# One scan instruction over two rows of states in a two-layer sequence model, with decays in PSUM and SBUF

## The chip, the cores and the metric

The kernel runs on one core of a Trainium2 chip. A core has five engines that run their own instruction streams and meet at semaphores: TensorE (matmuls and transposes, into PSUM), VectorE, ScalarE, GpSimd (no access to PSUM) and SyncE, which here only issues DMAs. The metric is the device time of one execution in microseconds (us). It is given as the median of three runs; the traces come from one profiled execution, whose own time stands beside its span.

## The reference, cut to what matters

Eight sequences of 1024 tokens with 512 features go through a conditioned linear-attention layer (layer 0) and then a conditioned state-space layer (layer 1). The change is in layer 1 alone. There the rows are gathered by a list of indices that lie, with these inputs, all below 512, so only the first 512 positions of each sequence have to be computed (the branch `first_chunk`). The core of the layer, for each sequence, 1024 inner channels d and 16 states s:

```python
A = -jnp.exp(A_log)                                  # [1024, 16]
dt = jax.nn.softplus(dtr @ W_dt + b_dt)              # [t, 1024]
def step(hst, inp):
    dt_t, B_t, C_t, x_t = inp
    dA = jnp.exp(dt_t[:, :, None] * A)               # the decay
    hst = hst * dA + (dt_t * x_t)[:, :, None] * B_t[:, None, :]
    y = jnp.einsum('bds,bs->bd', hst, C_t)
    return (hst, y)
...
y = jnp.transpose(ys, (1, 0, 2)) + xm * D_param
y = y * jax.nn.silu(z)
return y @ W_out
```

## The kernel before

Layer 0 takes the first third of the time and is not touched. In layer 1 the inner channels lie on partitions in eight groups j of 128, the 512 time steps lie along the free dimension. A **row** is one (j, s) pair, 128 partitions by 512 steps; a batch has 8 x 16 = 128 rows, and a **unit** U is four rows that share s and the half of the j. There are 32 units in a batch and 256 in all. `n` counts rows within a batch, `N` rows in all.

What is done for one row or unit:

- **Multiply** (GpSimd, `inputs`, L1866): the products (dt x)B of a unit's four rows in one operation of 128x2048, written to a place of the ring `hs` of four units (`RING = 4`). It waits until TensorE has turned all tiles of the unit four back (`turned`).
- **Decay** (ScalarE, `decays`, L1673): one Exp of 128x512 for each row, into one of three PSUM banks (`decay_banks`, banks 3 to 5), three rows ahead of the scan; it waits until the scan three rows back is done.
- **Scan** (VectorE, `scan`, L2029): the recurrence over 512 steps, in place in `hs`, with the decay from its PSUM bank. One instruction for each row.
- **Turn** (TensorE, `states_turned`, L1435): tile t of a unit is four 128x128 transposes that bring 128 time steps onto the partitions, into one of two PSUM banks. Tile t needs that tile t-2 was read.
- **Add** (VectorE, `add_states`, L2047, for tiles 0 to 2): multiply by C and add to `acc`. Tile 3 is scaled by ScalarE (`scale_state`, L1689) and added by a DMA that GpSimd issues (`pool_state`, L1904). `DVE_TILES = 3` sets this split.

The order on each engine is written out by hand: the function `turn(b)` of each engine runs over the 128 steps `n` and does at each one its part for row or tile `n`, and between them what other stages need at fixed steps (`XM_AT`, `DT_AT`, `Y_AT`, ...): the projections of the next batch, their taps (VectorE, L1997), SiLU and softplus on ScalarE, the gates, and a part of layer 0's output projection (`W_AT`), whose tiles come through `h_in` (three places). VectorE's adds run one step behind (`LAG = 1`), so in the unit of steps 4u to 4u+3 it scans unit u and adds the tiles of unit u-1. For each half batch GpSimd's queue has two more operations of 128x2048: L1847 (dt) and L1857 (dt times x).

The products of the other stages go through three **work banks** (6, 7 and 2), claimed in the order of `batch_places`. ScalarE computes softplus as an Exp and a Ln; Exp, Ln and SiLU are each in another set of tables, and a load of a set (`ACT_TABLE_LOAD`) is put ahead of an operation whose set is not there. `x_turned` (L1430) multiplies x by a diagonal matrix of D, eight of which VectorE makes once at the layer's start (L2187).

## Time and profile before

| | us |
|---|---|
| median of 3 runs | 3135.99 |
| lowest and highest | 3134.64, 3136.06 |
| the profiled execution, its own time | 3136.52 |
| its span in the trace | 3134.7 |
| busy: TensorE, VectorE, GpSimd, ScalarE | 2724.0, 2404.3, 1868.2, 1615.8 |
| first and last scan start | 1086.8, 3075.3 |

A busy time is the time in which an engine has an instruction under way. In the rows, a group has its busy time in us and the mean duration of one in ns, then the engine's idle time just ahead of the group and what ended it (the releaser). In a timeline the second number is the duration of the entry; an instruction's record may start while the one ahead of it is finishing, so two that run back to back overlap a little. "PE" is TensorE, "DVE" VectorE, "ACT" ScalarE, "POOL" GpSimd.

### The profile page before, as it was taken

To read this page: it belongs to the slowest core of one execution; us is meant where nothing else is said; L and a number is where in the kernel's file an instruction comes from. 1 tells how busy PE (TensorE), PEld (TensorE's weight loads), DVE (VectorE), ACT (ScalarE), POOL (GpSimd) and SP (SyncE) were. 2 spreads that over 40 slices of the span, in tenths; PEclk is the share of its full clock that TensorE was granted. 3 is DMA by queue.
4 is the path that set the end of the run, shared out by engine and by line. 5 is a ranking of instruction groups with operands and counts; after the bars stand their busy time and mean duration, and the time that the engine had idled before them with its cause. 6 is when DMAs were issued, how large, how long until landed. Compare 5 with 4: busy or idle time off the path is not lost. (4 is left out here: it accounts for less than half of the span.)

```text
span 3134.7 us, 32596 instructions
## 1 busy us (share of the span) xinstructions
PE 2724.0 (87%) x11066; PEld 1530.8 (49%) x11066; DVE 2404.3 (77%) x3090; ACT 1615.8 (52%) x2336; POOL 1868.2 (60%) x821
## 2 busy tenths in 40 slices
PE   7999999999999777988978888887897897888974
PEld 3556466456555344554544454444454454445542
DVE  3455445455544499989999999989998999999993
ACT  1222123223322466775775766776676577577550
POOL 0112111212113186887897898798799798789892
PEclk9999999999999778989989989999999998998976
DMA  6012022212215344454664664565566466456563
GB/s 207 7 54 74 27 101 88 88 54 89 85 65 164 107 96 99 108 118 114 142 154 104 152 152 105 140 157 112 128 158 132 105 157 142 111 139 144 146 136 72
DMA packets 261595, 355.28 MB, mean 113 GB/s; under 512 B 21597, under 2 KB 115937, under 8 KB 261434
## 3 DMA queue, kind: packets, MB, share of 16 engines
q1 hardware_dynamic: 202200, 246.46, 25.6%
q0 software_dynamic: 55680, 105.93, 19.6%
q8 instruction: 84, 1.38, 0.2%
q10 hardware_dynamic: 3554, 0.88, 0.1%
q14 instruction: 77, 0.63, 0.1%
HBM read 215.56 MB, written 71.58 MB: 92 GB/s over the span
## 5 line engine op out<-in xcount | busy, mean ns | idle before, releaser
L1866 POOL TENSOR_TENSOR hs<-slots,b_wide 128x2048 f32<-128x2048 f32 x256 | 1227.3, 4806 | 322.0 <-PE bank L1435 244.5
L2029 DVE TENSOR_TENSOR_SCAN hs<-bank,hs 128x512 f32<-128x512 f32 x1024 | 1219.7, 1208 | 48.5 <-ACT bank L1673 43.9
L1673 ACT ACTIVATE bank<-dt,decay 128x512 f32<-128x512 f32 x1024 | 700.4, 692 | 570.3 <-DVE hs L2029 568.9
L1435 PE MATMUL bank<-ident,hs 128*128 128x128 f32 x4096 | 681.1, 294 | 310.4 <-DVE acc L2047 240.8
L1435 PEld LDWEIGHTS bank<-ident,hs 128*128 128x128 f32 x4096 | 507.1, 150 | 848.0 <-DVE acc L2047 319.5
L2047 DVE SCALAR_TENSOR_TENSOR acc<-bank,c_t,acc 128x512 f32<-128x512 f32 x772 | 560.9, 727 | 62.7 <-PE bank L1435 60.6
L1388 PE MATMUL bank<-h_t,w_in 128*128 128x512 f32 x1024 | 509.3, 604 | 1.0 <-ACT h_t L1600 1.0
L1904 POOL DMA_DIRECT2D acc<-scaled x252 | 270.3, 1073 | 31.5 <-DMA acc<-scaled 19.3
L1483 PE MATMUL bank<-w_y,zs 128*128 128x512 f32 x512 | 253.0, 600 | 0.8 <-DVE zs L2148 0.8
L1399 PE MATMUL bank<-w_out,h_in 128*128 128x512 f32 x448 | 234.2, 649 | 1.3 <-ACT dt L1647 1.3
L711 PE MATMUL bank<-z_t,w_k 128*128 128x512 f32 x512 | 221.2, 592 | 0.9 <-ACT z_t L810 0.9
L711 PE MATMUL bank<-rows,z_t 128*128 128x512 f32 x512 | 221.1, 592 | 0.0
L711 PE MATMUL bank<-w_v,z_t 128*128 128x512 f32 x512 | 221.0, 592 | 0.0
L1388 PEld LDWEIGHTS bank<-h_t,w_in 128*128 128x128 f32 x1024 | 169.7, 194 | 82.6 <-issue 82.6
L868 POOL TENSOR_TENSOR x_rs<-x_var,mhalf 128x8 f32<-128x8 f32 x7 | 11.5, 1647 | 330.8 <-DVE x_var L298 330.8
L1689 ACT ACTIVATE scaled<-bank,c_t 128x512 f32<-128x512 f32 x252 | 169.7, 674 | 50.1 <-PE bank L1435 40.8
L873 POOL TENSOR_TENSOR qy<-qy,q_top 128x512 f32<-128x512 f32 x64 | 68.8, 1075 | 185.8 <-DVE q_top L945 185.8
L861 POOL TENSOR_TENSOR y_rs<-y_var,mhalf 128x8 f32<-128x8 f32 x8 | 15.9, 1992 | 254.6 <-DVE y_var L298 254.6
L813 ACT ACTIVATE k_t<-k_t,k_top 128x1024 f32<-128x1024 f32 x32 | 36.8, 1149 | 250.0 <-DVE k_top L915 250.0
L1997 DVE SCALAR_TENSOR_TENSOR slots<-bank,taps,slots 128x511 f32<-128x511 f32 (+2 forms) x192 | 142.1, 740 | 22.4 <-ACT slots L1613 19.9
L711 PEld LDWEIGHTS bank<-w_v,z_t 128*128 128x128 f32 x512 | 97.3, 190 | 122.5 <-issue 122.5
L711 PEld LDWEIGHTS bank<-z_t,w_k 128*128 128x128 f32 x512 | 96.7, 190 | 119.8 <-issue 118.6
(160 smaller groups left out, 3171.3 us busy)
## 6 DMA issues: line engine op xcount, KB each, us to landing
b_wide<-b_rows SPq DMA_DIRECT2D x256, 256.0 KB, 3.6
acc<-scaled POOLq DMA_DIRECT2D x252, 256.0 KB, 4.9
w_in<-in_L_cond_W_in SPq DMA_DIRECT2D x128, 256.0 KB, 3.3
z<-in_x SPq DMA_DIRECT2D x8, 2048.0 KB, 8.8
res<-in_x SPq DMA_DIRECT2D x8, 2048.0 KB, 9.7
h_tiles<-h_t SPq DMA_DIRECT2D x56, 256.0 KB, 3.4
h_in<-h_tiles SPq DMA_DIRECT2D x56, 256.0 KB, 4.8
x_rows<-w_part POOLq DMA_DIRECT2D x28, 512.0 KB, 8.9
```

What stands on the lines that cost most here:

```text
L711: last = nc.tensor.matmul(out[:, :], stationary(k), moving(k), start=(k == 0), stop=(k == blocks - 1))
L1388: last = nc.tensor.matmul(work_bank(place, stage, m)[:, :], w_in[:, m % W_IN_RING, k, :], h_t[:, place.par, k, :], start=(k == 0), stop=(k ...
L1399: last = nc.tensor.matmul(work_bank(place, "W", i)[:, :], h_in[:, w % W_RING, k, :], g.w_out[:, k, :], start=(k == 0), stop=(k == KD - 1))
L1435: last = nc.tensor.transpose(bank[:, j * P:(j + 1) * P], hs[:, slot, j, t * P:(t + 1) * P], ident[:, :])
L1483: last = nc.tensor.matmul(work_bank(place, "out", t)[:, :], zs[:, j, t * P:(t + 1) * P], w_y[:, j, :], start=(j == 0), stop=(j == KI - 1))
L1673: nc.scalar.activation(decay_banks[N % 3][:, :], dt[:, H % 2, j, :], ACT.Exp, scale=g.decay[:, 4 * (H % 2) + j, s:s + 1]).then_inc(da_read ...
L1689: nc.scalar.activation(scaled[:, U % SCALED_RING, t - DVE_TILES, :], state_banks[t % 2][:, :], ACT.Copy, scale=c_t[:, U // UNITS % 2, t, U ...
L1866: nc.gpsimd.tensor_tensor(hs[:, U % RING, :, :], slots[:, H % SLOTS, :, :], b_wide[:, U % B_RING, :].unsqueeze(1).to_broadcast([P, 4, CHUNK]),
L1904: nc.gpsimd.dma_start(acc[:, U // STATE % 2, DVE_TILES:, :], scaled[:, U % SCALED_RING, :, :], accum_op=ALU.add).then_inc(state_pooled, DMA)
L1997: nc.vector.scalar_tensor_tensor(row[:, back:], bank[:, 0:CHUNK - back], w, row[:, back:], ALU.mult, ALU.add).then_inc(empties(place, "xm" ...
L2029: nc.vector.tensor_tensor_scan(block, decay_banks[N % 3][:, :], block, 0.0, ALU.mult, ALU.add).then_inc(scanned, 1)
L2047: nc.vector.scalar_tensor_tensor(part, state_banks[t % 2][:, :], scale, part, ALU.mult, ALU.add).then_inc(summed, 1)
```

## The change

- **Paired scan.** `scan_pair` replaces `scan` in `turn`: one instruction over two neighbouring rows, 128x1024, at even steps. So that the second row starts from zero, the decay at each row's first step is zero: `clear_first` writes these zeros once, and `decays` writes elements 1 to 511 of each row only.
- **Decays in two pairs.** Rows 0 and 1 of a unit take their decays from a PSUM tensor of two banks (banks 3 and 4), rows 2 and 3 from `decay_pair` in SBUF. ScalarE runs four rows ahead (`LEAD`), and a row's decay is written once the pair two back is scanned.
- **Common tables.** After each SiLU the set that has both Exp and Ln is loaded at once; Exp and Ln then need no load between them.
- **Fourth work bank.** Bank 5 joins the work banks.
- **Room in SBUF.** Only two D diagonals are kept (`DIAG_RING`); ScalarE makes each again for every batch (`diagonal`, at `DIAG_AT`), and `x_turned` waits for it. `h_in` has two places in place of three, and its loads (`H_IN_AT`) are issued later.
- `tiles_of` now reads a table, with `THREE_TILES = 16`; as `U % STATE` is always below 16 it returns 3 as before, and the extra wait in `pool_state` never applies.

The diff, cut to its core:

```diff
+THREE_TILES = 16
+LEAD = 4
-W_RING = 3
+DIAG_RING = 2
+W_RING = 2
+DIAG_AT = (100, 103, 112, 114, 120, 122, 17, 20)
-H_IN_AT = (-1, 2, 5, 7, 24, 27, 30, 31)
+H_IN_AT = (3, 5, 7, 8, 27, 30, 31, 32)
...
-    places = [Place(b, b, b % 2, 2 * b, 0, {}, 3) for b in range(BATCH)]
+    places = [Place(b, b, b % 2, 2 * b, 0, {}, 4) for b in range(BATCH)]
...
+    return 3 if U % STATE < THREE_TILES else 2
...
+        decay_sb = sb("decay_pair", [P, 2 * CHUNK])
-        state_banks, decay_banks, work_banks = banks[0:2], banks[3:6], [banks[6], banks[7], banks[2]]
+        state_banks, decay_banks, work_banks = banks[0:2], banks[3:6], [banks[6], banks[7], banks[2], banks[5]]
+        decay_pairs = [g.decay_pair[:, :], decay_sb[:, :]]
...
             def x_turned(place, j):
                 out = claimed(pe, place, "init", j)
+                need(pe, d_ready, KI * place.it + j + 1)
...
-                    need(pe, scanned, 4 * (U + 1))
+                    need(pe, scanned, 2 * (U + 1))
...
+            def exp_and_log_tables():
+                nc.scalar.preload_act_table_set("natural_log_exp_and_others")
+            def diagonal(j):
+                nc.scalar.activation(d_diag[:, j % DIAG_RING, :], ident[:, :], ACT.Copy, scale=column(g, "L1_cond_D_param", j)).then_inc(d_ready, 1)
...
-                need(act, scanned, N - 2)
-                nc.scalar.activation(decay_banks[N % 3][:, :], dt[:, H % 2, j, :], ACT.Exp,
+                need(act, scanned, N // 2 - 1)
+                at = N % 2 * CHUNK
+                nc.scalar.activation(decay_pairs[N // 2 % 2][:, at + 1:at + CHUNK], dt[:, H % 2, j, 1:], ACT.Exp,
                                      scale=g.decay[:, 4 * (H % 2) + j, s:s + 1]).then_inc(da_ready, 1)
...
-                    if N + 3 < BLOCKS * BATCH:
-                        decays(N + 3)
+                    if N + LEAD < BLOCKS * BATCH:
+                        decays(N + LEAD)
...
+            def clear_first():
+                for pair in decay_pairs:
+                    nc.vector.memset(pair.rearrange("p (r t) -> p r t", t=CHUNK)[:, :, 0:1], 0.0).then_inc(first_cleared, 1)
+            def scan_pair(N):
+                need(dve, da_ready, N + 2)
                 if N % 4 == 0:
                     need(dve, inputs_ready, N // 4 + 1)
-                block = hs[:, N // 4 % RING, N % 4, :]
-                nc.vector.tensor_tensor_scan(block, decay_banks[N % 3][:, :], block, 0.0, ALU.mult, ALU.add).then_inc(scanned, 1)
+                rows = hs[:, N // 4 % RING, N % 4:N % 4 + 2, :].rearrange("p r t -> p (r t)")
+                nc.vector.tensor_tensor_scan(rows, decay_pairs[N // 2 % 2], rows, 0.0, ALU.mult, ALU.add).then_inc(scanned, 1)
...
-                    scan(N)
+                    if n % 2 == 0:
+                        scan_pair(N)
...
-                nc.vector.tensor_scalar(d_diag[:, j, :], ident[:, :], column(g, "L1_cond_D_param", j), None, ALU.mult).then_inc(d_ready, 1)
```

VectorE's order in a stretch of the first batches' scans where little stands between, before (`hs<-bank,hs` is a scan, `acc<-...` an add; the listing prints a scan under another operation's name):

```order
L2047 SCALAR_TENSOR_TENSOR acc<-bank,c_t,acc 128x512
L2029 SCALAR_TENSOR_TENSOR hs<-bank,hs 128x512 x2
L2047 SCALAR_TENSOR_TENSOR acc<-bank,c_t,acc 128x512
L2029 SCALAR_TENSOR_TENSOR hs<-bank,hs 128x512
L2047 SCALAR_TENSOR_TENSOR acc<-bank,c_t,acc 128x512
L2029 SCALAR_TENSOR_TENSOR hs<-bank,hs 128x512
L2047 SCALAR_TENSOR_TENSOR acc<-bank,c_t,acc 128x512
L2029 SCALAR_TENSOR_TENSOR hs<-bank,hs 128x512 x2
```

The same engine after, with the scans of 1024 elements from `bank` and from `decay_pair` in turn:

```order
L2080 SCALAR_TENSOR_TENSOR hs<-decay_pair,hs 128x1024
L2098 SCALAR_TENSOR_TENSOR acc<-bank,c_t,acc 128x512 x2
L2080 SCALAR_TENSOR_TENSOR hs<-bank,hs 128x1024
L2098 SCALAR_TENSOR_TENSOR acc<-bank,c_t,acc 128x512
L2080 SCALAR_TENSOR_TENSOR hs<-decay_pair,hs 128x1024
L2098 SCALAR_TENSOR_TENSOR acc<-bank,c_t,acc 128x512 x2
```

A unit was scan, scan, add, scan, add, scan, add; it is now a pair, an add, a pair and two adds.

ScalarE around the Exp (L1653) and Ln (L1658) of softplus, before:

```order
L1673 ACTIVATE bank<-dt,decay 128x512
L1625 COPY zs<-bank 128x512
L1673 ACTIVATE bank<-dt,decay 128x512
L1658 ACT_TABLE_LOAD
L1658 ACTIVATE dt<-dt 128x2048
L1673 ACT_TABLE_LOAD
L1673 ACTIVATE bank<-dt,decay 128x512 x2
```

and after, where they are L1674 and L1679:

```order
L1715 ACTIVATE scaled<-bank,c_t 128x512
L1699 ACTIVATE bank<-dt,decay 128x511
L1683 ACTIVATE d_diag<-ident,cols 128x128
L1643 COPY zs<-bank 128x512
L1699 ACTIVATE bank<-dt,decay 128x511
L1679 ACTIVATE dt<-dt 128x2048
L1699 ACTIVATE decay_pair<-dt,decay 128x511 x2
L1715 ACTIVATE scaled<-bank,c_t 128x512
```

The two table loads around Ln are gone, a diagonal stands between the copies, and the decays come in twos for a bank and for `decay_pair`.

## Rows read from the trace of the kernel before

**Rows 1.** Busy time in one stretch: us, PE, PEld, DVE, ACT, POOL.

```profile
1290.00:2790.00 1500.00, 1276.36 (x5429) 713.79 (x5430) 1414.31 (x1606) 1019.71 (x1444) 1258.15 (x501) 0.95 0.57 132
```

**Rows 2.** The page's costliest groups: the multiply and the decays.

```profile
L1866 POOL TENSOR_TENSOR hs<-slots,b_wide 128x2048 f32<-128x2048 f32 x256 | 1227.3, 4806 | 322.0 <-PE bank L1435 244.5
...
L1673 ACT ACTIVATE bank<-dt,decay 128x512 f32<-128x512 f32 x1024 | 700.4, 692 | 570.3 <-DVE hs L2029 568.9
```

**Rows 3.** Waits in 1290 to 2790: total us, times, longest.

```profile
POOL hs L1866 <- PE bank L1435: 193.9, 98, 3.5
...
DVE acc L2047 <- PE bank L1435: 44.7, 44, 3.1
DVE hs L2029 <- ACT bank L1673: 34.3, 36, 2.2
```

**Rows 4.** All scans (ns min/median/max); scans, then multiplies, in the stretch.

```profile
L2029 DVE TENSOR_TENSOR_SCAN hs<-bank,hs x1024: 1184/1210/1225, 1086.8 to 3075.3; 128x512 f32<-128x512 f32 x171
...
1290.00:2790.00 1500.00, 903.65 (x760) 0.95 0.57 132
...
1290.00:2790.00 1500.00, 903.50 (x190) 0.95 0.57 132
```

**Rows 5.** Timeline of VectorE: start us, us, instruction.

```profile
1208.06 1.21 DVE L2029 TENSOR_TENSOR_SCAN hs<-bank,hs 128x512 f32<-128x512 f32 x1
1209.19 0.73 DVE L2047 SCALAR_TENSOR_TENSOR acc<-bank,c_t,acc 128x512 f32<-128x512 f32 x1
1209.83 1.21 DVE L2029 TENSOR_TENSOR_SCAN hs<-bank,hs 128x512 f32<-128x512 f32 x1
```

**Rows 6.** Timeline of TensorE, GpSimd and VectorE at two adds of tile 1.

```profile
1209.97 1.11 PE L1435 MATMUL bank<-ident,hs 128*128 128x128 f32 x4 [0.66 <-DVE acc L2047]
...
1206.73 0.88 POOL L1904 DMA_DIRECT2D acc<-scaled  x1
1211.24 4.51 POOL L1866 TENSOR_TENSOR hs<-slots,b_wide 128x2048 f32<-128x2048 f32 x1 [3.64 <-PE bank L1435]
...
1117.23 0.72 DVE L2047 SCALAR_TENSOR_TENSOR acc<-bank,c_t,acc 128x512 f32<-128x512 f32 x1
...
1118.00 0.66 PE L1435 MATMUL bank<-ident,hs 128*128 128x128 f32 x4 [2.11 <-DVE acc L2047]
...
1118.82 4.55 POOL L1866 TENSOR_TENSOR hs<-slots,b_wide 128x2048 f32<-128x2048 f32 x1 [1.78 <-PE bank L1435]
```

**Rows 7.** L371, all and one, with the GpSimd operation beside it.

```profile
L371 DVE SCALAR_TENSOR_TENSOR shift<-mv,rs x7: 1101/4464/4483, 1114.2 to 2628.5; 128x4 f32<-128x4 f32 x7
...
1614.32 4.44 DVE L371 SCALAR_TENSOR_TENSOR shift<-mv,rs 128x4 f32<-128x4 f32 x1
1618.69 1.21 DVE L2029 TENSOR_TENSOR_SCAN hs<-bank,hs 128x512 f32<-128x512 f32 x1
...
1613.59 5.14 POOL L1866 TENSOR_TENSOR hs<-slots,b_wide 128x2048 f32<-128x2048 f32 x1
```

**Rows 8.** Two lengths of a plain operation; two scans back to back.

```profile
L2014 DVE TENSOR_TENSOR dt<-dt,rows x1: 2293/2293/2293, 1077.1 to 1077.1; 128x2048 f32<-128x2048 f32 x1
...
L943 DVE TENSOR_TENSOR qy<-bank,q_bias x64: 681/692/692, 119.1 to 964.5; 128x512 f32<-128x512 f32 x64
...
1164.95 2.33 DVE L2029 TENSOR_TENSOR_SCAN hs<-bank,hs 128x512 f32<-128x512 f32 x2
```

**Rows 9.** Groups by line and form: table loads, the eight diagonals.

```profile
L1620 ACT ACT_TABLE_LOAD x28 | 35.9, 1283 | 0.5
...
L1620 ACT ACTIVATE slots<-slots 128x1024 f32<-128x1024 f32 x32 | 33.8, 1057 | 10.1 <-DVE slots L1997 9.8
...
L1658 ACT ACT_TABLE_LOAD x16 | 20.5, 1283 | 0.3
...
L1631 ACT ACT_TABLE_LOAD x16 | 20.5, 1283 | 0.3
...
L2187 DVE TENSOR_SCALAR d_diag<-ident,cols x8: 281/281/286, 1019.7 to 1021.0; 128x128 f32<-128x128 f32 x8
```

More of the change, by code:

```diff
@@ L194, in tiles_of, with scaled_before @@
 def tiles_of(U):
-    return DVE_TILES if U < DIRECT else CT
+    if U >= DIRECT:
+        return CT
+    return 3 if U % STATE < THREE_TILES else 2
+TILES_BEFORE = [0, *itertools.accumulate(tiles_of(U) for U in range(BATCH * UNITS))]
 def sums_before(U):
-    return DVE_TILES * U + (CT - DVE_TILES) * max(U - DIRECT, 0)
+    return TILES_BEFORE[U]
+def scaled_before(U):
+    return CT * U - TILES_BEFORE[U]
 def need(eng, semaphore, value):
@@ L240, in sb, with ps @@
             return whole.enter_context(nc.sbuf_tensor(name, shape, dt))
-        g.banks = [whole.enter_context(nc.psum_tensor(f"bank{i}", [P, 512], F32)) for i in range(8)]
+        def ps(name, n):
+            return whole.enter_context(nc.psum_tensor(name, [P, n * 512], F32))
+        first_banks, g.decay_pair, last_banks = [ps(f"bank{i}", 1) for i in range(3)], ps("bank34", 2), [ps(f"bank{i}", 1) for i in range(5, 8)]
+        g.banks = [*first_banks, *(g.decay_pair[:, i * 512:(i + 1) * 512] for i in range(2)), *last_banks]
         g.ident = sb("ident", [P, P])
@@ L1032, in layer1 @@
         fin_free, idx_in_ready, mod_ready = (sem(n) for n in ("fin_free", "idx_in_ready", "mod1_ready"))
-        work_ready, work_empty = ([sem(f"work_{n}{i}") for i in range(3)] for n in ("ready", "empty"))
+        work_ready, work_empty = ([sem(f"work_{n}{i}") for i in range(4)] for n in ("ready", "empty"))
         end_turned, end_gated = sem("end_turned"), sem("end_gated")
@@ L1428, in x_turned @@
                 out = claimed(pe, place, "init", j)
+                need(pe, d_ready, KI * place.it + j + 1)
                 for t in range(CT):
-                    last = nc.tensor.matmul(out[:, t * P:(t + 1) * P], x_row(place, j)[:, t * P:(t + 1) * P], d_diag[:, j, :], start=True, stop=True)
+                    last = nc.tensor.matmul(out[:, t * P:(t + 1) * P], x_row(place, j)[:, t * P:(t + 1) * P], d_diag[:, j % DIAG_RING, :], start=True, stop=True)
                 last.then_inc(fills(place, "init", j), 1)
@@ L1713, in turn @@
                             start_sum(place if j >= 4 else after, j)
+                    for j, at in enumerate(DIAG_AT):
+                        if n == at:
+                            if more or j >= 6:
+                                diagonal(j)
                     if n == 2 and prev:
                         silu_z(PLACES[b - 1], 1)
+                        exp_and_log_tables()
                     for j, at in enumerate((5, 6, 10, 11)):
@@ L1755, in turn @@
                         silu_z(place, 0)
+                        exp_and_log_tables()
                     if n == 78 and not more:
                         silu_z(place, 1)
+                        exp_and_log_tables()
             def first_chunk():
                 place = PLACES[0]
+                for j in range(DIAG_RING):
+                    diagonal(j)
                 for i in range(KD):
@@ L1774, in first_chunk @@
                     start_sum(place, j)
-                for N in range(3):
+                    diagonal(j + DIAG_RING)
+                act.wait_ge(first_cleared, 2)
+                for N in range(LEAD):
                     decays(N)
@@ L1804, in body @@
                             log_dt(place, half)
+                        for j in range(DIAG_RING):
+                            diagonal(j)
                         for j in range(KI):
                             start_sum(place, j)
+                            if j + DIAG_RING < KI:
+                                diagonal(j + DIAG_RING)
                         for k in range(BLOCKS):
@@ L1900, in pool_state @@
             def pool_state(U):
-                need(pool, state_scaled, (CT - DVE_TILES) * (U + 1))
+                need(pool, state_scaled, scaled_before(U + 1))
                 need(pool, *pooled(U))
-                nc.gpsimd.dma_start(acc[:, U // STATE % 2, DVE_TILES:, :], scaled[:, U % SCALED_RING, :, :], accum_op=ALU.add).then_inc(state_pooled, DMA)
+                n = tiles_of(U)
+                if U % STATE == THREE_TILES and U % STATE > 0:
+                    need(pool, summed, sums_before(U))
+                nc.gpsimd.dma_start(acc[:, U // STATE % 2, n:, :], scaled[:, U % SCALED_RING, 0:CT - n, :], accum_op=ALU.add).then_inc(state_pooled, DMA)
             def turn(b):
@@ L2066, in add_states @@
                     need(dve, summed, sums_before(U - 1) + min(t, tiles_of(U - 1) - 1) + 1)
-                if t >= DVE_TILES:
+                if U >= DIRECT and t >= 2:
                     need(dve, *pooled(DIRECT))
@@ L2135, in first_chunk @@
             def first_chunk():
+                clear_first()
                 for m in range(KI):
@@ L2183, in both_chunks @@
                 batches(dve, body)
-            end_banks = [banks[3], banks[4], banks[5], banks[0]]
-            for j in range(KI):
-                nc.vector.tensor_scalar(d_diag[:, j, :], ident[:, :], column(g, "L1_cond_D_param", j), None, ALU.mult).then_inc(d_ready, 1)
-            dve.wait_ge(d_ready, KI)
+            end_banks = [banks[3], banks[4], banks[0], banks[1]]
             either(dve, first_chunk, both_chunks)
```

18 lines of the change are left out of this document (8 added, 10 removed).

## Prediction

> **What bounds the kernel now.** I read the busy time by stretch first. In the middle of the second layer, 1290 to 2790 us, VectorE works 1414 of 1500 us, TensorE 1276, GpSimd 1258, ScalarE 1020 [rows 1]. 760 scans fall in it [rows 4], so 190 units of four rows: 7.89 us for a unit, of which VectorE is busy 7.44. VectorE is the bound, and its 0.45 us idle per unit is mostly waiting for a turned tile (44.7 us) and for a decay (34.3 us) [rows 3]. GpSimd is not saturated: it waits 193.9 us for TensorE to have turned a unit four back and so to free a place of the ring `hs` [rows 3]. That row is why GpSimd's multiply starts when it does, and it matters below. The whole stretch of scans runs from 1086.8 to 3075.3+1.2 us [rows 4], 1989.7 us or 7.77 us a unit over 256 units.
>
> One unit on VectorE, by start times: a scan holds the engine 1.13 us before an add can start (1208.06 to 1209.19), an add 0.64 us (to 1209.83) [rows 5]. Four scans and three adds are 4 x 1.13 + 3 x 0.64 = 6.44 us; the remaining 1.00 us of 7.44 is taps, gates and statistics.
>
> **The paired scan by itself.** 1024 scans become 512 of twice the length. No row shows one of 1024 elements. An ordinary two-input operation takes 2293 ns for 2048 elements and 692 for 512 [rows 8]: (2293 - 692)/1536 = 1.042 ns an element and 158 ns fixed, though one of them reads PSUM and the other doesn't. With that fixed part the scan of 1210 ns [rows 4] takes 2.055 ns an element, so a pair takes 158 + 1024 x 2.055 = 2262 ns, and holds the engine 0.08 less (as 1.21 against 1.13 shows): 2.18 us in place of 2.26. Gain 0.08 x 512 = 41 us. The ends are 0 (the fixed part is paid per row) and 0.16 a pair, 82 us (all that a scan has over 512 x 2.055 = 1052 ns is saved). I take 0.08, which also fits the two scans that run back to back in 2.33 us [rows 8].
>
> The Trainium skill ("VectorE: DVE Perf Modes", section on the TRN2 errata) gives a fixed 120 cycles with a PSUM source and 58 with SBUF alone. By that figure a PSUM pair would save 0.125 us and the sum would be some 64 us; the rows above show less of it exposed, and I stay with them.
>
> **Where the second pair's decays lie.** Rows 0 and 1 of a unit take their decays from PSUM (call that pair P), rows 2 and 3 from `decay_pair` in SBUF (S). S then has two tensor inputs in SBUF, decay and `hs`; none of today's scans has. The trace shows what such an operation does beside GpSimd: L371 is a 128x4 operation with two SBUF inputs, and it takes 1101 to 4483 ns, median 4464 [rows 7]. The one at 1614.32 ends at 1618.76; GpSimd's multiply beside it started at 1613.59 and ended at 1618.73 [rows 7]. It did nothing until the multiply was over. The scan with its decay in PSUM is untouched: 1184 to 1225 ns over all 1024 [rows 4], though GpSimd multiplies more than half of the time (903.5 of 1500 us) [rows 4].
>
> The Trainium skill ("SBUF — State Buffer", section "SBUF: two separate sides") states it as an exclusive lock between a VectorE operation with two SBUF inputs and a GpSimd operation that reads SBUF: whichever starts first has it for the whole instruction. It names no exception for scans, and it speaks against this change; the trace agrees on VectorE's side (4464 ns), and no row shows GpSimd held.
>
> So the question is where S meets the multiply (4.53 us when it starts from idle [rows 6]). Follow one unit. VectorE's order is now P, add 0, S, add 1, add 2. Add 1 frees the bank for TensorE's tile 3, and tile 3 frees the `hs` place, which lets the multiply for the unit four later start. From the start of add 1 to the start of the multiply the trace has 2.05 us (1209.19 to 1211.24, TensorE's four transposes in 1.11) and 1.59 us (1117.23 to 1118.82, transposes in 0.66) [rows 5, 6]; I take 1.82. The chain from S to the next S is then
>
> 2.18 (S) + 1.82 (add 1, tile 3) + 4.53 (the multiply) = 8.53 us, 8.30 to 8.76 by the two ends.
>
> VectorE would have been ready for the next S after 2.18 + 0.64 + 0.64 + 2.18 + 0.64 = 6.28 us plus 1.00 of other work, 7.28. The multiply has begun at 4.00, so S finds it running and waits. GpSimd has 8.53 - 4.53 - 0.88 (its DMA issue [rows 6]) = 3.1 us to spare per unit, so it doesn't fall back out of this order by small extras. Every unit then costs 8.53 where it costs 7.77.
>
> **The sum.** 256 x 8.53 = 2184 us for the scans, against 1989.7: plus 194. The 41 us of the pairing are in it. On the profiled run's 3136.5 us (span 3134.7; the median is 3136.0, so the two agree) that is **3330 us**.
>
> **The other edits**, at nothing in this sum:
> - Common tables. The load before each of 16 Ln goes [rows 9] and the one before the next Exp: 32 x 1.28 = 41 us of ScalarE. It waits 569 us for scans already [rows 2], so this reaches the end only through the 34.3 us in which a scan waits for a decay. SiLU keeps its two loads, one before it and one after, 44 times [rows 9].
> - Diagonals. 64 copies of 128x128 join ScalarE; VectorE took 281 ns for one [rows 9]. ScalarE's nearest, 512 wide, takes 692 [rows 2]. So 18 to 44 us, hidden in the same idle time. TensorE now waits for a diagonal before it turns x, with the state tiles queued behind it; each is written several steps ahead. Eight VectorE operations at the start, 2.2 us, go.
> - Decay buffers. A row's decay could be written after the scan three back: some 2.9 us for one Exp of 0.69. Now a pair's two, 1.38, must fit into P or S and an add, 2.18 + 0.64 = 2.8. The slack falls from 2.2 to 1.4 us, and a SiLU block of 3.6 us (two loads of 1.28 and the operation of 1.06 [rows 9]) overruns either. Worth 0.8 us in each of 44 such places, up to 35 us, but S's wait of 8.53 - 7.28 = 1.25 us covers it.
> - Tile 3 and the next unit's tile 0 are both wanted within add 2 and P, 2.8 us in place of 4.0; TensorE's extra products fall in there. The same wait covers it; without that cover it is up to 0.5 us a unit.
> - The fourth work bank only takes waits away. `h_in` shrinks to two places, loads are issued later; the cover is about a unit (7.8 us) against a load of some 5. No `acc` tile changes engine: the new table still gives VectorE three.
>
> **The rivals.**
> 1. *The scan goes first.* If S starts while GpSimd is between multiplies, the multiply starts at S's end, runs beside add 1, add 2, P and add 0, and is over at 6.71, before VectorE wants S at 7.28. Then a unit costs 7.28 and some waits, 7.35: 256 x 7.35 = 1882, 108 less: **3029**. For it: GpSimd still has its 0.88 to issue, so it is ready at 7.59, and a plain unit is at S by 6.28. Against it: three taps (1.9 us), the statistics or a SiLU block carry a unit past 7.59. The multiply then slips in, costs 4.53, and from there the ring makes the order above hold. The two other 2048-wide GpSimd operations per half batch can throw it back. Chance 0.10.
> 2. *A mix* of the two orders, half of the units each: (8.53 + 7.35)/2 = 7.94, 43 us more: **3179**. Chance 0.17. It decides by sign: the point of no change is 7.77, where two of three units go by rival 1.
> 3. *The scan isn't held at all.* L371 is another operation, and a scan takes twice as long an element as a plain one (2.055 against 1.042 ns), so it may leave the port free in between. Against it: L371 needs almost nothing of the port and was held all the same. Then the 41 us remain: **3095**, 3055 to 3136 by the ends of the pair's cost and by more waiting for decays. Chance 0.11.
> 4. *Worse than forecast*: each time the multiply slips in, the unit costs 2.18 + 4.53 + 0.88 + 4.53 = 12.1 us, 3.6 more. Three a batch are 86 us: **3416**. Chance 0.04.
> The forecast has 0.58, with a range of its own from 3265 (8.30 a unit, less some SiLU waits gone) to 3410 (8.76 and a few slips).
>
> **How the numbers follow.** The likeliest is 3330. The range 3080 to 3410 leaves out rival 1, rival 4 and the edges of the others, 0.18 in all. Under 0.2% (about 6 us) a measurement can't tell from no change. Faster: rivals 1 and 3, 0.21. Same: 0.02, slices of 2 and 3. Slower: 0.77.
>
> **What would show it.** The 256 scans with `decay_pair` as input would have records far above the 256 from a bank: forecast 2.3 us plus a wait of about 1.2 to 2.2 us, ending 2.2 us after a multiply's end; those from a bank near 2.26. GpSimd's idle time ahead of its multiply would grow well over 322 us [rows 2], VectorE's idle gaps shrink. Equal records for both kinds would mean rival 3; short SBUF scans with GpSimd multiplies starting at their ends rival 1. The forecast is wrong if the multiply waits for S more often than S for it, since it takes the order from one unit and not from a count.

## The result and the profile after

The changed kernel takes 3445.68 us (median of 6 runs, 3438.12 to 3448.11), the kernel before, run beside it, 3135.31 (3131.81 to 3136.32): a ratio of 1.0989, 95% interval 1.0975 to 1.1003. It is slower by 310 us. The forecast had the sign and the mechanism, 3330 and a range up to 3410; the time lies 36 us above the range.

The three costliest groups of VectorE after the change (line, engine, operation, output and inputs, count, busy us, mean ns of one, idle time ahead of them and its releasers), and the source line of the scans (ns minimum, median and maximum, first and last start in us):

```profile
L2080 DVE TENSOR_TENSOR_SCAN hs<-decay_pair,hs 128x1024 f32<-128x1024 f32 x256 | 949.6, 3709 | 16.9 <-ACT decay_pair L1699 16.9
L2080 DVE TENSOR_TENSOR_SCAN hs<-bank,hs 128x1024 f32<-128x1024 f32 x256 | 582.4, 2275 | 6.4 <-POOL hs L1908 4.7 <-ACT bank L1699 1.8
L2098 DVE SCALAR_TENSOR_TENSOR acc<-bank,c_t,acc 128x512 f32<-128x512 f32 x772 | 548.1, 730 | 76.7 <-PE bank L1453 74.2 <-DMA acc<-scaled 1.2
...
L2080 DVE TENSOR_TENSOR_SCAN hs<-bank,hs x256: 2258/2274/2290, 1084.5 to 3379.1; 128x1024 f32<-128x1024 f32 x128
L2080 DVE TENSOR_TENSOR_SCAN hs<-decay_pair,hs x256: 2276/3550/11336, 1086.7 to 3382.6; 128x1024 f32<-128x1024 f32 x128
```

Both lines are one instruction of one size on one engine. From PSUM (P) all 256 lie between 2258 and 2290 ns; from SBUF (S) the shortest is 2276 and the mean 3709, so each S is held 1.43 us on average, 366 us in all. The scans now run from 1084.5 to some 3385, 8.99 us a unit where [rows 4] give 7.77. VectorE counts as busy while it is held, so the hold doesn't show as idle time:

```profile
1300.00:2800.00 1500.00, 1162.11 (x4775) 656.01 (x4774) 1439.12 (x1063) 886.83 (x1292) 1157.93 (x437) 0.91 0.51 116
```

That is the stretch of [rows 1] moved by 10 us (busy us of TensorE, its loads, VectorE, ScalarE, GpSimd, then TensorE's granted clock): VectorE's busy time has risen from 1414 to 1439 us, TensorE's has fallen from 1276 to 1162 and GpSimd's from 1258 to 1158, since all others wait for the scans. TensorE's granted clock has gone from 0.95 to 0.91. The multiply stands as in [rows 2]:

```profile
L1908 POOL TENSOR_TENSOR hs<-slots,b_wide 128x2048 f32<-128x2048 f32 x256 | 1170.4, 4572 | 554.6 <-PE bank L1453 473.6
```

GpSimd idles 554.6 us ahead of it where it idled 322.0.

The chain itself is in the timeline (start us, duration us), VectorE first and then GpSimd:

```profile
2024.19 3.98 DVE L2080 TENSOR_TENSOR_SCAN hs<-decay_pair,hs 128x1024 f32<-128x1024 f32 x1
2028.09 1.38 DVE L2098 SCALAR_TENSOR_TENSOR acc<-bank,c_t,acc 128x512 f32<-128x512 f32 x2
2029.39 2.27 DVE L2080 TENSOR_TENSOR_SCAN hs<-bank,hs 128x1024 f32<-128x1024 f32 x1
...
2021.51 4.51 POOL L1908 TENSOR_TENSOR hs<-slots,b_wide 128x2048 f32<-128x2048 f32 x1 [3.27 <-PE bank L1453]
2025.97 0.86 POOL L1950 DMA_DIRECT2D acc<-scaled  x1
2029.68 4.51 POOL L1908 TENSOR_TENSOR hs<-slots,b_wide 128x2048 f32<-128x2048 f32 x1 [2.85 <-PE bank L1453]
```

The multiply ends at 2026.02 and S at 2028.17, 2.15 us later, as if S had started only then. Add 1 starts at 2028.09, the next multiply 1.59 us after it, and so on: 8.17 us from one multiply to the next. It is the chain that the forecast made, with its three terms at 2.07 (from the multiply's end to add 1), 1.59 and 4.51 us where it had 2.18, 1.82 and 4.53.

### The profile page after: what moved, and what is told of

The parts are those of the page before. It is cut to its first block and busy times, and to the rows that moved or that the text cites. A ratio compares the mean times of both kernels' runs of the same rounds, so it can differ in the third digit from the quotient of the medians.

```text
span 3442.6 us, 32234 instructions
## 1 busy us (share of the span) xinstructions
PE 2787.2 (81%) x11066; PEld 1574.9 (46%) x11066; DVE 2727.5 (79%) x2572; ACT 1600.7 (46%) x2372; POOL 1950.5 (57%) x821
## 5 line engine op out<-in xcount | busy, mean ns | idle before, releaser
L1908 POOL TENSOR_TENSOR hs<-slots,b_wide 128x2048 f32<-128x2048 f32 x256 | 1170.4, 4572 | 554.6 <-PE bank L1453 473.6
L1453 PE MATMUL bank<-ident,hs 128*128 128x128 f32 x4096 | 707.8, 304 | 575.1 <-DVE acc L2098 519.3
L1453 PEld LDWEIGHTS bank<-ident,hs 128*128 128x128 f32 x4096 | 533.8, 155 | 1128.2 <-DVE acc L2098 711.8
L2080 DVE TENSOR_TENSOR_SCAN hs<-decay_pair,hs 128x1024 f32<-128x1024 f32 x256 | 949.6, 3709 | 16.9 <-ACT decay_pair L1699 16.9
L1699 ACT ACTIVATE decay_pair<-dt,decay 128x511 f32<-128x511 f32 x512 | 351.6, 716 | 634.1 <-DVE hs L2080 633.6
L2098 DVE SCALAR_TENSOR_TENSOR acc<-bank,c_t,acc 128x512 f32<-128x512 f32 x772 | 548.1, 730 | 76.7 <-PE bank L1453 74.2
L2080 DVE TENSOR_TENSOR_SCAN hs<-bank,hs 128x1024 f32<-128x1024 f32 x256 | 582.4, 2275 | 6.4 <-POOL hs L1908 4.7
L1405 PE MATMUL bank<-h_t,w_in 128*128 128x512 f32 x1024 | 530.0, 625 | 1.0 <-ACT h_t L1618 1.0
L1699 ACT ACTIVATE bank<-dt,decay 128x511 f32<-128x511 f32 x512 | 342.0, 685 | 277.5 <-DVE hs L2080 277.1
L1950 POOL DMA_DIRECT2D acc<-scaled x252 | 225.5, 895 | 3.5 <-DMA acc<-scaled 1.8
L2043 DVE SCALAR_TENSOR_TENSOR slots<-bank,taps,slots 128x511 f32<-128x511 f32 (+2 forms) x192 | 142.0, 740 | 20.6 <-ACT slots L1631 18.1
L951 DVE TENSOR_TENSOR values<-bank,v_bias 128x512 f32<-128x512 f32 x64 | 44.2, 691 | 140.1 <-PE bank L727 140.1
```

The lines of the kernel that those rows point to most:

```text
L1405: last = nc.tensor.matmul(work_bank(place, stage, m)[:, :], w_in[:, m % W_IN_RING, k, :], h_t[:, place.par, k, :], start=(k == 0), stop=(k ...
L1453: last = nc.tensor.transpose(bank[:, j * P:(j + 1) * P], hs[:, slot, j, t * P:(t + 1) * P], ident[:, :])
L1699: nc.scalar.activation(decay_pairs[N // 2 % 2][:, at + 1:at + CHUNK], dt[:, H % 2, j, 1:], ACT.Exp, scale=g.decay[:, 4 * (H % 2) + j, s:s ...
L1908: nc.gpsimd.tensor_tensor(hs[:, U % RING, :, :], slots[:, H % SLOTS, :, :], b_wide[:, U % B_RING, :].unsqueeze(1).to_broadcast([P, 4, CHUNK]),
L1950: nc.gpsimd.dma_start(acc[:, U // STATE % 2, n:, :], scaled[:, U % SCALED_RING, 0:CT - n, :], accum_op=ALU.add).then_inc(state_pooled, DMA)
L2043: nc.vector.scalar_tensor_tensor(row[:, back:], bank[:, 0:CHUNK - back], w, row[:, back:], ALU.mult, ALU.add).then_inc(empties(place, "xm" ...
```

## The experiments

Durations "a unit" below are counted from the traces, from the end of one S to the end of the next, and numbered by the first of the two, as means over the batches in the middle of the run. "Plain" are in the changed kernel the units below 8.8 us, and elsewhere those of the commonest short length. "Held" is what an S lasts beyond its free 2.28 us. All ratios are to the kernel before on the same chip.

### What does the pairing give if nothing is held?

The part that is left out, for both kernels and for one without pairs (L1908 is `inputs`, in the kernel before L1866; the two time-step operations are cut to their first step):

```diff
-                nc.gpsimd.tensor_tensor(hs[:, U % RING, :, :], slots[...], b_wide[...], ALU.mult).then_inc(inputs_ready, 1)
+                nc.gpsimd.memset(hs[:, U % RING, :, :], 0.5).then_inc(part_filled, 1)
+                need(pool, part_filled, U + 1)
+                nc.gpsimd.memset(hs[:, U % RING, :, :], 0.5).then_inc(inputs_ready, 1)
```

> The kernel before with GpSimd made to read almost nothing from SBUF: its multiply is left out (two memsets of the same place of hs stand in its place, the second waiting for the first, 3.7 us together), and its two operations on dt work on the first time step only. This is the control for the next two: no kernel of the three has a scan that could be held. Every theory: VectorE stays the bound, about 3120 us (3100 to 3135).

> The changed kernel with the same parts of GpSimd's work left out. Theory A (the hold is the whole loss; all else in the change gives what was forecast): below the control by 41 to 75 us, 3050 to 3080 us. Theory B (the pairs' coarser order also makes VectorE wait for TensorE's tiles, as its 150 us of waits in the three-memset run suggests): about the control or above it, 3110 to 3180 us. Rival (SBUF as a source makes a scan slower even when nothing holds it): SBUF scans clearly above 2.28 us.

> The changed kernel with one scan for each row again, decays in the same places, and the same parts of GpSimd's work left out. It has all other parts of the change (tables, fourth bank, diagonals, lead). Theory A: above the paired one by 41 us for the pairing. Theory B: below the paired one or equal to it, since the tiles' windows are those of before. In both, common tables and the fourth bank put it at or a little below the control: 3085 to 3120 us.

Measured: the kernel before in this form 3108.85 us (ratio 0.9919, 0.9891 to 0.9948), the changed one 3060.32 (0.9765, 0.9736 to 0.9793), the one with four single scans and the same places of decays 3099.21 (0.9889, 0.9860 to 0.9917). The scans, first of the changed kernel in this form, then of the one without pairs:

```profile
L2082 DVE TENSOR_TENSOR_SCAN hs<-bank,hs x256: 2264/2278/2291, 1081.1 to 2992.6; 128x1024 f32<-128x1024 f32 x128
L2082 DVE TENSOR_TENSOR_SCAN hs<-decay_pair,hs x256: 2265/2280/2292, 1083.3 to 2996.1; 128x1024 f32<-128x1024 f32 x128
...
L2090 DVE TENSOR_TENSOR_SCAN hs<-bank,hs 128x512 f32<-128x512 f32 x512 | 599.0, 1205 | 7.8 <-ACT bank L1700 4.0 <-POOL hs L1911 3.8
L2090 DVE TENSOR_TENSOR_SCAN hs<-decay_pair,hs 128x512 f32<-128x512 f32 x512 | 620.9, 1213 | 0.0
```

Without GpSimd's readers a scan from SBUF takes what one from PSUM takes. The change is then 48.5 us faster than its control: 38.9 by the pairs (3099.21 - 3060.32), 9.6 by the other edits. All three times lie where they were expected (for the changed one, theory A). So the changed kernel loses 310 + 49 = 359 us to something that disappears with GpSimd's readers, and the 366 us by which the S records exceed 2.28 us are nearly as much.

### Is it GpSimd's reading?

Three memsets in place of the multiply write the same 2048 elements three times but read nothing; GpSimd's two time-step operations are whole. It was run once.

> Leaves out the multiply: in its place GpSimd writes a constant to the same place of hs three times (three memsets, each waiting for the one before), so it writes SBUF but reads nothing there. Theory (the hold is between an operation with two SBUF inputs and a GpSimd operation that reads SBUF): the SBUF scans that run beside it take 2.28 us as the others do, except those beside the few GpSimd operations that still read; the total falls to 3110 us or below, depending on how long three memsets take. Rival (writing alone takes the port too): SBUF scans still show waits of one memset's length, 3150 to 3400 us.

Measured: 3232.15 us.

```profile
L2083 DVE TENSOR_TENSOR_SCAN hs<-decay_pair,hs x256: 2265/2280/7341, 1088.1 to 3170.6; 128x1024 f32<-128x1024 f32 x128
...
1300.00:2800.00 1500.00, 1229.52 (x5209) 704.99 (x5207) 1357.24 (x1172) 955.09 (x1401) 1386.66 (x845) 0.93 0.56 126
```

The median S is 2280 ns, though GpSimd is busy for 1386.66 of 1500 us, mostly writing `hs`. Only 19 S are held more than 0.1 us, and all 19 stood beside one of the two time-step operations, which still read. So writing does not hold a scan. The time is above the 3110 us of the theory, which had left open how long three memsets take: 5.8 us, more than the 4.5 of the multiply, so GpSimd, busy for 92% of the stretch, probably became the bound. The time of this run decides nothing; its S records do.

### Is it the pair, or where the decays lie?

> The changed kernel with one scan instruction for each row again, decays in the same four places (rows 2 and 3 of each unit from SBUF), everything else kept. Theory (chain through the SBUF scan that stands before add 1): only one scan of 1.13 us stands between the multiply's end and add 1, the other follows 0.64 us later and gets in before the next multiply, so the chain is 1.13 + 1.77 + 4.53 = 7.4 us in place of 8.3; VectorE itself needs 7.4 on average. With GpSimd's extra jobs 8.2 us a unit: 3250 us (3190 to 3320). Rival (pairing is a gain of 41 us by itself and the placement costs what it costs): 3446 + 41 = 3487 us.

The edit: `scan_pair` becomes one scan per row, with the decays where the change puts them.

```diff
-                rows = hs[:, N // 4 % RING, N % 4:N % 4 + 2, :].rearrange("p r t -> p (r t)")
-                nc.vector.tensor_tensor_scan(rows, decay_pairs[N // 2 % 2], rows, 0.0, ALU.mult, ALU.add).then_inc(scanned, 1)
+                row = hs[:, N // 4 % RING, N % 4, :]
+                at = N % 2 * CHUNK
+                nc.vector.tensor_tensor_scan(row, decay_pairs[N // 2 % 2][:, at:at + CHUNK], row, 0.0, ALU.mult, ALU.add).then_inc(scanned, 1)
```

Measured: 3435.98 us (1.0979, 1.0954 to 1.1004), almost the changed kernel. Neither expectation holds: the time is 186 us above the one and 51 below the other.

```profile
L2088 DVE TENSOR_TENSOR_SCAN hs<-decay_pair,hs 128x512 f32<-128x512 f32 x512 | 969.3, 1893 | 0.0
L2088 DVE TENSOR_TENSOR_SCAN hs<-bank,hs 128x512 f32<-128x512 f32 x512 | 597.5, 1201 | 6.8 <-POOL hs L1908 4.7 <-ACT bank L1699 2.1
```

1893 against the free 1213 ns, 512 times, is 348 us held. Without any pair the kernel loses about what the changed one loses. The place of the decays does it. The plain unit, 7.19 us, is near the expected 7.4; what the expectation had too low is the rest. It let the scan of row 3 get in ahead of the next multiply, but 43 of these 256 scans did not and were held 3.6 us each, 155 of the 348 us.

> The changed kernel with no decay in SBUF: rows 0 and 1 stay one pair from two PSUM banks, rows 2 and 3 are scans of one row each, both from the third decay bank; three work banks and a lead of three rows as in the kernel before; common tables and the other edits stay. No scan has two operands in SBUF, so by the theory (such a scan is held by a GpSimd operation that reads SBUF) none is held: every single scan 1.18 to 1.23 us, the pair 2.28, the multiply at its 4.5 to 4.6. What it keeps is half of the pairs' gain (39 us in the runs with the two parts left out, so 20) and the 10 us of the other edits: 3105 at best. Against it: the exponential of row 3 can start only when row 2's scan has left the bank, 0.69 us and its wait against the 0.64 us of one addition between them: 0.1 to 0.3 us a unit, 25 to 75 us. Forecast 3140 (3105 to 3180). Rival, that what costs the changed kernel its time is the pairing and the order that it gives the engine, and not the place of the decays: near 3290, half way between the two kernels.

```diff
-LEAD = 4
+LEAD = 3
-        decay_sb = sb("decay_pair", [P, 2 * CHUNK])
+                if N % 4 >= 2:
+                    need(dve, da_ready, N + 1)
+                    row = hs[:, N // 4 % RING, N % 4, :]
+                    nc.vector.tensor_tensor_scan(row, banks[5][:, :], row, 0.0, ALU.mult, ALU.add).then_inc(scanned, 1)
+                    return
```

Measured: 3306.86 us (1.0546, 1.0531 to 1.0560), far from 3140, and the rival's 3290 is nearer. But the rival's reason is not in the trace:

```profile
L2080 DVE TENSOR_TENSOR_SCAN hs<-bank,hs 128x512 f32<-128x512 f32 x512 | 623.1, 1217 | 43.7 <-ACT bank L1701 24.2
L2085 DVE TENSOR_TENSOR_SCAN hs<-bank,hs 128x1024 f32<-128x1024 f32 x256 | 584.3, 2282 | 111.6 <-ACT bank L1698 106.9 <-POOL hs L1909 4.7
L2103 DVE SCALAR_TENSOR_TENSOR acc<-bank,c_t,acc 128x512 f32<-128x512 f32 x772 | 563.1, 730 | 104.6 <-PE bank L1451 102.0 <-DMA acc<-scaled 2.1
...
ACT bank L1701 <- DVE hs L2080: 801.1, 280, 8.3
```

No scan is held (1217 and 2282 ns). The time went into idle gaps of VectorE: 155 us ahead of its scans, mostly for decays, and 105 ahead of its adds, where the kernel before has 48.5 and 62.7. ScalarE waits 801.1 us (last row: total, times, longest) at the Exp of rows 2 and 3, for their one bank, and what stands behind that Exp in its queue comes later, the next pair's decays among it. So three decay banks are too few for a pair and two rows, which the expectation priced at 25 to 75 us. The run confirms that scans with PSUM decays are not held, pair or single, though GpSimd reads as before; it also shows why the change needs the room in SBUF. Which part of its 171 us falls to which wait was not tried apart.

### Does the order decide, and what upsets it?

> The two decay pairs change places: rows 0 and 1 of a unit take their decays from SBUF, rows 2 and 3 from PSUM. The number of scans with two SBUF inputs stays 256. Theory (place in the chain): the SBUF scan now follows add 1 and add 2 directly and is ready 1.28 us after add 1 starts, before the next multiply (1.59 us after it), so it goes first and the multiply starts at its end. A plain unit then costs 2.20 + 4.53 = 6.7 us up to about 7.3, where it costs 8.26 now; in the units with taps or statistics behind add 1 (some 8 of 32) the multiply still gets in and the unit costs about 12. Mean about 8.3 us a unit, 3285 us in all (3230 to 3340). Rival (only the number and length of the SBUF scans counts, not their place): within 1% of the changed kernel, 3446 us.

```diff
-        decay_pairs = [g.decay_pair[:, :], decay_sb[:, :]]
+        decay_pairs = [decay_sb[:, :], g.decay_pair[:, :]]
```

Measured: 3641.66 us (1.1628, 1.1609 to 1.1647), slower still. Where nothing stands between, the unit is near what was expected, 6.7 us (VectorE, then GpSimd):

```profile
2024.51 2.50 DVE L2080 TENSOR_TENSOR_SCAN hs<-decay_pair,hs 128x1024 f32<-128x1024 f32 x1
...
2031.07 2.41 DVE L2080 TENSOR_TENSOR_SCAN hs<-decay_pair,hs 128x1024 f32<-128x1024 f32 x1
...
2041.39 10.89 DVE L2080 TENSOR_TENSOR_SCAN hs<-decay_pair,hs 128x1024 f32<-128x1024 f32 x1
...
2026.01 5.32 POOL L1908 TENSOR_TENSOR hs<-slots,b_wide 128x2048 f32<-128x2048 f32 x1 [0.30 <-PE bank L1453]
...
2040.11 4.54 POOL L1908 TENSOR_TENSOR hs<-slots,b_wide 128x2048 f32<-128x2048 f32 x1
2044.56 1.02 POOL L1950 DMA_DIRECT2D acc<-scaled  x1
2045.21 4.92 POOL L1908 TENSOR_TENSOR hs<-slots,b_wide 128x2048 f32<-128x2048 f32 x1
```

6.56 us from S to S. Here GpSimd is held too: the multiply at 2026.01 takes 5.32 us, 0.8 more than usual, and S was running until 2027.01. Then the order breaks: S starts at 2041.39, one multiply is running, a second follows it, S ends at 2052.28, 2.15 us after the second. The expectation had this for some 8 of 32 units, at 12 us. There are 13 above 11 us in a batch, units 1, 4, 9 and 26 take 16 to 18 us, and 32 S in the program outlast two or three GpSimd operations, which no expectation had priced.

> The changed kernel with one wait more: GpSimd's multiply for unit U waits until the second scan pair of unit U-2 is done, so it can never start ahead of the SBUF scan that it would hold. Theory: no SBUF scan is held by a multiply that started before it could; a plain unit costs max(2.20 + 4.53, what VectorE needs) = 7.0 to 7.3 us. GpSimd has less lead, so each of its longer extra jobs (4.8 us operations of dt, the gather; some five a batch) now stalls the first scan of a unit by some 3 us. Mean about 7.8 us a unit: 3150 us (3080 to 3200). Rival (GpSimd's throughput or something else than the hold sets the time, less lead only makes it worse): over 3446 us.

```diff
+                need(pool, scanned, 2 * (U - 1))
                 nc.gpsimd.tensor_tensor(hs[:, U % RING, :, :], slots[...], b_wide[...], ALU.mult).then_inc(inputs_ready, 1)
```

Measured: 3315.81 us (1.0587, 1.0569 to 1.0604). Better than the changed kernel by 130 us, worse than expected by 166. Plain units take 6.93 us. The S mean is still 3043 ns: 107 S are held more than 0.1 us, 25 of them by a time-step operation; the new wait keeps a multiply behind one S, but not from meeting the next. Units 1, 5, 9 and 26 of a batch, near GpSimd's other jobs, take 11.9 to 13.6 us.

> The changed kernel with GpSimd's two operations of 128x2048 on dt cut to the first time step (their work on the other 511 is left out); the multiplies are whole. Theory (GpSimd's extra jobs come on top of the chain of scan, tile 3 and multiply and cost about their own length less little): units 5, 9, 26 and 29 of a batch fall from 10.2 to 12.2 us to the plain 8.3, some 12 us a batch, 88 in all: 3358 us (3330 to 3385). Rival (GpSimd has 3.1 us to spare in a unit, and takes up these jobs mostly there): 3410 to 3440 us.

```diff
-                nc.gpsimd.tensor_tensor(part, part, positive, ALU.add).then_inc(dt_ready, 1)
+                nc.gpsimd.tensor_tensor(part[:, :, 0:1], part[:, :, 0:1], positive[:, :, 0:1], ALU.add).then_inc(dt_ready, 1)
```

(and the multiplication after it likewise). Measured: 3364.45 us (1.0735, 1.0702 to 1.0768), 81 us less, where 88 were expected. Unit 5 of a batch falls from 12.2 to 8.6 us and unit 29 from 11.1 to 8.2, as the theory has it; unit 9 falls only to 9.1, and unit 26 hardly (10.2 to 10.0).

> The changed kernel with one step of VectorE moved: per unit P, addition 0, addition 1, S, addition 2, in place of P, addition 0, S, additions 1 and 2. The multiply starts 1.59 us after addition 1 as before, but S now stands right behind that addition and starts first, with nothing of GpSimd running unless an extra job is. Theory: the order is then S 2.3 (held little or not), the multiply beside additions and P, a unit of 7.6 to 8.0 us where nothing extra stands on GpSimd, and holding only beside its extra jobs: 3300 (3200 to 3400). Rival, that the multiply is late from the unit before and always meets S, whatever stands ahead of it: 3420 to 3480.

```diff
+                if 0 <= U < DIRECT:
+                    return ((), (0, 1), (), (2,))[step]
```

Measured: 3401.75 us (1.0849, 1.0832 to 1.0865), 44 us below the changed kernel and 2 above the expected range, so the theory's 3300 was missed. Half of the units take 8.1 us or less, many 6.9, but units 4 and 25 take 19.1 and 18.1. One of them (VectorE, then GpSimd):

```profile
1871.61 13.99 DVE L2080 TENSOR_TENSOR_SCAN hs<-decay_pair,hs 128x1024 f32<-128x1024 f32 x1
...
1868.42 5.14 POOL L1908 TENSOR_TENSOR hs<-slots,b_wide 128x2048 f32<-128x2048 f32 x1
1872.90 1.56 POOL L1950 DMA_DIRECT2D acc<-scaled  x1
1873.51 5.49 POOL L1889 TENSOR_TENSOR dt<-dt,rows 128x2048 f32<-128x2048 f32 x1
1877.98 5.47 POOL L1908 TENSOR_TENSOR hs<-slots,b_wide 128x2048 f32<-128x2048 f32 x1
```

S is ready at 1871.61 and ends at 1885.60, 2.15 us after the end (1883.45) of the third GpSimd operation. The operation on dt and the next multiply both have records that start after that of S, and both went first.

> The kernel with addition 1 ahead of S, and GpSimd's two operations on the time steps (the addition and the multiplication of 2048 elements, each once a half batch) cut to the first time step, so their result is left out nearly whole. With addition 1 ahead of S and these two whole, 3401.8 was measured, with units of 19.1 and 18.1 us where they run, 11 us above their neighbours, and of 11 two and three units behind: there one record of S is 13.7 us long, so S seems to be held by such an operation and then by the multiply queued behind it. Theory, that these two operations are what keeps this order from working: 22 us in each of 8 batches go, and 5 of their followers' 8, so 3402 - 216 = 3186 (3150 to 3240). Rival, that they cost what they cost in the changed kernel, 80 us, and the units are long there for another reason: 3320.

The edit is the last two together. Measured: 3197.01 us (1.0194, 1.0177 to 1.0211) where 3186 was expected and the rival had 3320. Units 4 and 25 are at 8.1 and 8.2 us.

```profile
L2080 DVE TENSOR_TENSOR_SCAN hs<-decay_pair,hs x256: 2271/2281/9505, 1085.2 to 3132.2; 128x1024 f32<-128x1024 f32 x128
```

The median S is free, and 104 us of holding are left. In this order two operations of a half batch, 30 in the program, cost 205 us, some 6.8 us each; in the changed kernel's order 81 us, 2.7 each. What is left long is unit 0 (13.0 us), where GpSimd gathers rows by four indirect DMAs ahead of its multiply, and units 2 (11.0) and 18 (10.2), whose S is free.

### One of the other edits alone

> The kernel before with one edit of the change alone: the tables of ScalarE's functions common to its stages. In the kernel before the loads of tables stand in ScalarE's waits at the stages' borders. Theory, that they are covered there only in part and are some of the 10 us that the edits beside the pairs gave: 3120 to 3133. Rival, that they are hidden behind other work, as the prediction had it: no change, 3133 to 3137.

```diff
+            def exp_and_log_tables():
+                nc.scalar.preload_act_table_set("natural_log_exp_and_others")
...
                         silu_z(PLACES[b - 1], 1)
+                        exp_and_log_tables()
```

(likewise after the other SiLU blocks). Measured: 3118.60 us (0.9944, 0.9931 to 0.9958), 18 us faster than the kernel before (13 to 22 by the interval), the fastest run here that leaves nothing out.

```profile
L2036 DVE TENSOR_TENSOR_SCAN hs<-bank,hs 128x512 f32<-128x512 f32 x1024 | 1218.5, 1208 | 24.0 <-ACT bank L1676 19.3 <-POOL hs L1873 4.7
```

The scans' waits for decays fall from 43.9 (all of them; [rows 3] has the 34.3 of the middle stretch) to 19.3 us.

## Why the prediction was right in kind and too low

- **The pair by itself**: forecast 2262 ns and a gain of 41 us; measured 2275 to 2280 and 38.9. Right.
- **Held by reading from SBUF**: right. The S records, the untouched P records, memsets that do not hold and half pairs from PSUM that are not held all say so.
- **The Trainium skill** ("SBUF — State Buffer", "SBUF: two separate sides") was borne out on both engines, scans included: S is held by a multiply (3709 ns in place of 2280), and a multiply by S (5.32 us in place of 4.51). The Trainium skill's page "VectorE: DVE Perf Modes", section on the TRN2 errata, was not: without holding, a pair from PSUM (2278 ns) and one from SBUF (2280) take the same, so its difference of fixed cost does not show in a scan.
- **The chain of a plain unit**: forecast 8.53, 8.30 to 8.76. 185 of 255 units are plain, and their mean is 8.26 us, with 8.18 and 8.19 the commonest. The wait from add 1 to the multiply is in most of them the shorter one of [rows 6], 1.59 us, and in some 34 the longer one of about 2.05, where the unit takes 8.6. The unit was too high by 0.27 us: on all 256, 69 us.
- **The failed step** is "so it doesn't fall back out of this order by small extras. Every unit then costs 8.53". The order stays (195 of 256 S are held more than 0.1 us), but not every unit costs the same: the other 70 have a mean of 10.9 us, which makes 187 us in the program, and the sum had nothing for them. Two terms were missing.

  GpSimd's extra jobs. In 48 of the 70 units S is held, and they make 142 of the 187 us: units 0 (13.0 us; gather), 5 (12.2; addition on dt), 9 (11.0; dt times x), 26 (10.2; dt), 29 (11.1; dt times x) and some with smaller excesses. The 3.1 us to spare are there (2.85 measured), but a job of 5.0 to 5.9 us outlasts them, the multiply starts late by the rest, and S is held until that is over. The jobs are this long because they are held themselves: all 30 time-step operations started 0.6 to 1.7 us before an S ended, and ended 4.33 to 4.35 us after its end. The prediction had said that no row shows GpSimd held.

  VectorE's own work, taken as 1.00 us in every unit. It comes in lumps. In the other 22, units 2 (11.6 us), 18 (9.4) and most of 27 (9.8), S is free (2.28 us): VectorE has more to do there than the chain lasts, as in the kernel before, where the same units take 11.0, 10.0 and 9.0 us. They make 45 of the 187 us. The comparison of 8.53 with a mean of 7.28 hid them. Unit 2 has these entries among others:

```profile
1979.89 2.46 DVE L374 BATCH_NORM_STATS2 raw<-rows 128x6 f32<-128x512 f32 x4
1986.49 2.25 DVE L387 SCALAR_TENSOR_TENSOR shift<-mv,rs 128x4 f32<-128x4 f32 x1
1988.66 2.28 DVE L2080 TENSOR_TENSOR_SCAN hs<-decay_pair,hs 128x1024 f32<-128x1024 f32 x1
```

  And unit 5, where S is held (VectorE, then GpSimd):

```profile
2003.78 3.55 DVE L2080 TENSOR_TENSOR_SCAN hs<-decay_pair,hs 128x1024 f32<-128x1024 f32 x1
...
2012.00 7.54 DVE L2080 TENSOR_TENSOR_SCAN hs<-decay_pair,hs 128x1024 f32<-128x1024 f32 x1
...
2005.75 5.92 POOL L1889 TENSOR_TENSOR dt<-dt,slots 128x2048 f32<-128x2048 f32 x1
2011.63 1.22 POOL L1875 DMA_DIRECT2D x_rows<-w_part  x1
2012.41 4.97 POOL L1908 TENSOR_TENSOR hs<-slots,b_wide 128x2048 f32<-128x2048 f32 x1
```

  Add 1 starts at 2007.26 there, so the multiply could have started at 2008.85 and ended at 2013.4. It stands behind the operation on dt and a DMA issue and ends at 2017.38, 4 us later, and S, ready since 2012.00, ends at 2019.54. The prediction named these operations only as something that could restore the better order. So: 8.26 x 256 = 2115 us, plus 187, makes 2302 for the scans; the forecast had 2184 and the kernel before 1989.7. The 118 us between 2302 and 2184 are the miss of 116 (3446 against 3330).
- **Rival 4** came nearest: it had three slips a batch at 3.6 us, each a second multiply ahead of S. Of its mechanism there is a single case, an S that outlasts two reading operations. What came instead is about five extra jobs a batch, at 2.7 to 4.7 us, and two or three long units of VectorE. That its 3416 is the nearest of all times is partly luck. A loss above the forecast was weighed too low at 0.04, and the bound of 3410 with it.
- **Rivals 1 to 3** are out. Rival 1's short unit exists (6.93 us with the order forced or add 1 moved), and what the long units cost then is what these runs show. The scan is held, so rival 3 is out; it gives what it would have given only without readers, 3060 against 3109.
- **The other edits**: forecast at nothing, measured -10 us together and -18 for the tables alone, so the diagonals, the narrower `h_in` and the later decays may cost some 8 us; that was not tried alone, and compares runs with and without GpSimd's readers. In the changed kernel the S waits cover most of it, as was said: decays are waited for 18.7 us there.
- **What would show it**: S near 2.3 plus 1.2 to 2.2 us (2.28 + 1.43), S ending 2.2 us after a multiply's end (2.15), P near 2.26 (2.275), GpSimd's idle time well over 322 us (554.6): all came. The stated sign of being wrong, a multiply that waits for S more often than S for it, did not come (5 multiplies started while a free S ran, 195 S were held). VectorE's gaps shrank ahead of the scans (48.5 to 23.3 us), but not ahead of the adds, which wait 74.2 us for tiles where they waited 60.6.

The account of the whole: 3135 before, -49 for pairs and the other edits when nothing is held, +366 for holding by the S records, makes 3452; measured were 3446. Of the loss 81 us go with the two time-step operations.

## What to carry to other kernels

Before a buffer moves from PSUM to SBUF to make room for a larger instruction, ask whether the instruction then has two inputs in SBUF, and what GpSimd reads meanwhile. One such wait per unit is easy to chain together; price each extra GpSimd job on top, since it pushes back the operation for which the scan then waits. Idle time of GpSimd covers a job only up to its own length (2.85 us here, of a job of 5.9 that the scan has lengthened itself). Compare the chain with VectorE's work unit by unit, not with its mean. The order of the two engines can be improved by moving one small instruction (44 us here), but a margin of less than a microsecond (0.3 us with the pairs swapped, 0.9 with add 1 moved) does not survive a queue with other jobs in it.

## What the runs showed of the hardware

- A held S ends 2.15 us after the GpSimd operation that held it: 2.145 to 2.157 us for nine tenths of the 200 or so in the changed kernel. A free one takes 2.28, so at most 0.13 us of it is done ahead.
- GpSimd is held too, and as wholly: a multiply of 4.51 us that starts while S runs ends 4.3 to 4.5 us after S does (123 times with the pairs swapped, up to 6.6 us long). With the time-step operations cut to one step, all 30 still lasted 1.0 to 1.6 us and ended with the S beside them.
- A waiting scan is not let in between GpSimd operations that follow closely. With add 1 moved ahead, 16 scans outlasted two or three of them, up to 14.0 us. The Trainium skill ("SBUF — State Buffer", "SBUF: two separate sides") has whoever starts first hold the lock for the whole instruction; a multiply whose record starts later than that of the waiting S nevertheless goes first here, so by the records the order of starting does not decide.
- The issue of a DMA by GpSimd does not hold a scan by itself. In the traces of the changed kernel and of five of its variants (pairs swapped, order forced, narrow dt, add 1 first, both of these), 200 S start during an issue with the next reading operation a microsecond or more away, and all take 2.27 to 2.32 us. But of the 74 that start during an issue with a reading operation less than a microsecond away, 36 are held by it, though its record starts later (unit 5 above is one); of the 66 that start so near to one without an issue under way, none is.
- A scan costs (2275 - 1208)/512 = 2.08 ns an element and some 0.14 us fixed. With nothing held it is the same with the decay in SBUF (2280 and 1213 ns).
